# Three graph-convolution stages: slots' own rows loaded into the message tile first, gathered rows added to them by the indirect DMA

## The reference

```
def gcn_layer(h, W, b):
    hW = h @ W
    msg = norm * hW[row]                       # norm = dinv[row] * dinv[col]
    out = segment_sum(msg, col, num_segments=N)
    return out + b
h = relu(gcn_layer(x, W0, b0))                 # 128 -> 256
h = relu(gcn_layer(h, W1, b1))                 # 256 -> 256
h = gcn_layer(h, W2, b2)                       # 256 -> 128
x = layernorm(x + h)
```

## Time and profile before

| | us |
|---|---|
| median of 3 runs | 6531.18 (6519.85 to 6533.77) |
| the profiled execution, its own time | 6535.03 |
| its span in the trace | 6533.2 |
| first stage, from its first gather to the second stage's | 5422.0 to 5686.7 |
| second stage, likewise | 5686.7 to 6013.3 |
| third stage, to the end of the span | 6013.3 to 6533.2 |

### The profile page before, as it was taken

How to read it: one execution, slowest core, us unless ns; L and a number is a source line. 1 busy time by engine, 2 the same in 40 slices (tenths; PEclk the granted TensorE clock), 3 DMA queues, 4 the chain that set the end, 5 groups by cost and what they waited for, 6 DMA issues and landing times. The chain is left out here.

```text
span 6533.2 us, 85961 instructions
## 1 busy us (share of the span) xinstructions
PE 4769.7 (73%) x23527; PEld 3216.8 (49%) x23527; DVE 4268.8 (65%) x12858; ACT 3169.3 (49%) x7126; POOL 3968.9 (61%) x3991
## 2 busy tenths in 40 slices
PE   6899999889989843696435555556999996598221
PEld 4667776555558602596333333323666664465111
DVE  4788887433349745888895554556888886655554
ACT  3566665553346402554353455545888873364000
POOL 5566664654446477776676676674333336674777
PEclk9999999989999855696556776756999997799555
DMA  6999887887769623796556777765777776675332
GB/s 151 238 263 274 258 250 224 263 250 249 244 219 285 191 55 78 203 349 197 137 157 184 193 211 194 194 159 180 275 276 275 276 245 191 201 216 166 89 94 82
DMA packets 1135684, 1345.16 MB, mean 206 GB/s; under 512 B 137098, under 2 KB 822139, under 8 KB 1128938
## 3 DMA queue, kind: packets, MB, share of 16 engines
q1 hardware_dynamic: 1005066, 1085.70, 53.4%
q0 software_dynamic: 130144, 253.97, 16.1%
HBM read 659.31 MB, written 683.78 MB: 206 GB/s over the span
## 5 line engine op out<-in xcount | busy, mean ns | idle before, releaser
L1909 POOL DMA_INDIRECT jk_msg<-jk,idx_jk x588 | 554.8, 944 | 220.1 <-issue 174.1
L2173 POOL TENSOR_TENSOR rows_moved<-rows_x_in,w_lonely_row 128x512 f32<-128x512 f32 x98 | 152.5, 1557 | 561.3 <-DVE rows_x L722 537.0
L730 PE MATMUL jk_msg_ps<-ident,jk_msg 128*128 128x128 f32 x784 | 187.3, 383 | 418.8 <-DMA jk_msg<-jk,idx_jk 310.7
L1993 DVE TENSOR_TENSOR jk_msg_ps<-jk_msg_ps,jk_weight 128x512 f32<-128x512 f32 x196 | 137.1, 699 | 453.6 <-ACT jk_msg_ps L1948 343.8
L730 PEld LDWEIGHTS jk_msg_ps<-ident,jk_msg 128*128 128x128 f32 x784 | 123.9, 193 | 531.3 <-DMA jk_msg<-jk,idx_jk 410.0
L747 PE MATMUL sage_nodes_h_ps<-sage_nodes_h_t,w_ws 128*128 128x512 f32 x784 | 353.6, 594 | 0.0
L1930 PE MATMUL jk_h_ps<-jk_sum_t,w_jk_w 128*128 128x512 f32 x392 | 324.2, 923 | 27.9 <-DVE jk_sum_t L2010 26.5
L1249 DVE COPY sage_h<-sage_turn 128x512 f32<-128x512 f32 x98 | 67.7, 691 | 420.9 <-PE sage_turn L738 420.9
L2372 PE MATMUL gcn_end_sum_ps<-ident,gcn_end_rows 128*128 128x128 f32 x196 | 54.7, 434 | 384.4 <-DVE gcn_end_rows L2365 384.4
L945 ACT ACTIVATE sage_nodes_h_t<-sage_nodes_h_ps,w_b_c 128x512 f32<-128x512 f32 x392 | 247.7, 683 | 167.2 <-PE sage_nodes_h_ps L747 166.5
L610 POOL DMA_INDIRECT sage_msg<-h,idx x196 | 185.3, 945 | 230.9 <-ACT sage_weighted L1074 152.0
(11 more groups left out here) (455 smaller groups left out, 16104.9 us busy)
## 6 DMA issues: line engine op xcount, KB each, us to landing
h<-sage_nodes_h SPq DMA_DIRECT2D x196, 512.0 KB
h_t<-sage_h_t SPq DMA_DIRECT2D x98, 512.0 KB, 4.3
h<-sage_h SPq DMA_DIRECT2D x98, 512.0 KB, 3.5
jk_weight<-l_row SPq DMA_DIRECT2D x196, 256.0 KB
jk_t<-jk_h_t SPq DMA_DIRECT2D x196, 256.0 KB
rows_layers<-jk_t SPq DMA_DIRECT2D x49, 1024.0 KB, 5.8
r<-rows_h SPq DMA_DIRECT2D x98, 512.0 KB, 4.1
second_x_in<-u SPq DMA_DIRECT2D x147, 260.0 KB
```

What stands on the lines that cost most here:

```text
L730: mm = pe.transpose(ps[:, s * P:(s + 1) * P], rows[:, s, :], ident[:])
L1909: pool.indirect_dma_start(out=msg[:, j.number % deep, s, :], out_offset=None, in_=table, in_offset=bass.IndirectOffsetOnAxis(ap=index[:, g ...
L1993: dve.tensor_tensor(bank[:], bank[:], weight[:, j.number % 3, :], ALU.mult).then_inc(weighed.sem, 1)
L2173: pool.tensor_tensor(moved[:, g.b], x_in[:, g.number % 3], to_subs(W.lonely_row), ALU.add).then_inc(lonely_added.sem, 1)
```

## The change

The tiles `own` and `rows` and the function `vector_join` go. SP's own-row load now writes into `msg`; POOL waits for it, and then its four indirect DMAs add the gathered rows to what lies there. PE transposes straight from `msg` in the first and third stage; in the second ACT's `weigh` reads `msg` and writes a ring `rows` of two. `msg` has 8 buffers (6 in the second stage) and is freed by the transposes (by `weigh` in the second stage). SP issues the own loads further ahead.

```diff
+LOOP_DEEP, LOOP_DEEP_WIDE = 8, 6
@@ class LoopSums
-        self.depth, self.own_depth = DEEP if width == D else DEEP_WIDE, 3
+        self.depth = LOOP_DEEP if width == D else LOOP_DEEP_WIDE
...
-        self.own = ph.sb("own", [P, self.own_depth, SUB, width])
-        self.rows = ph.sb("rows", [P, 2, SUB, width])
...
+        self.scaled, self.freed = None, self.turned
+
+    def turn_from(self, rows, scaled):
+
+        self.rows, self.scaled, self.freed = rows, scaled, scaled
+
+    def sync_own(self, sp, g):
+        wait_for(sp, self.freed, g.lag(self.depth))
+        sp.dma_start(self.msg[:, g.number % self.depth], at(slot_rows(self.table), g)).then_inc(self.own_in.of(g), 16)
 
     def pool_fetch(self, pool, g):
-        pool_gather(pool, g, self.K.idx, self.joined, self.table, self.msg, self.arrived)
...
-    def vector_join(self, dve, g):
-        wait_for(dve, self.arrived, g)
-        wait_for(dve, self.own_in, g)
-        wait_for(dve, self.turned, g.lag(2))
-        dve.tensor_tensor(self.rows[:, g.b], self.msg[:, g.number % self.depth], self.own[:, g.number % self.own_depth], ALU.add).then_inc(self.joined.sem, 1)
...
+        wait_for(pool, self.own_in, g)
+        for s in range(SUB):
+            pool.indirect_dma_start(out=self.msg[:, g.number % self.depth, s, :], out_offset=None, in_=self.table,
+                                    in_offset=bass.IndirectOffsetOnAxis(ap=self.K.idx[:, cols(g, SUB, s, 1)], axis=0),
+                                    compute_op=ALU.add).then_inc(self.arrived.of(g), 16)
+
+    def tensor_turn(self, pe, g):
+        if self.scaled is None:
+            wait_for(pe, self.arrived, g)
+            rows = self.msg[:, g.number % self.depth]
+        else:
+            wait_for(pe, self.scaled, g)
+            rows = self.rows[:, g.b]
...
@@ gcn_first_block
-        run_groups(sp, EG, [(lambda g: sums.sync_own(sp, g), -2), (store, 2)])
+        run_groups(sp, EG, [(lambda g: sums.sync_own(sp, g), -6), (store, 2)])
...
@@ gcn_second_block
+    rows = ph.sb("rows", [P, 2, SUB, HID])
...
+    sums.turn_from(rows, weighed)
...
-        run_groups(sp, EG, [(lambda g: sums.sync_own(sp, g), -2), (store, 4)])
+        run_groups(sp, EG, [(lambda g: sums.sync_own(sp, g), -4), (store, 4)])
...
-            wait_for(act, sums.joined, g)
+            wait_for(act, sums.arrived, g)
+            wait_for(act, sums.turned, g.lag(2))
             for s in range(SUB):
-                ins = act.activation(sums.rows[:, g.b, s, :], sums.rows[:, g.b, s, :], ACT.Copy, scale=K.dinv[:, cols(g, SUB, s, 1)])
+                ins = act.activation(rows[:, g.b, s, :], sums.msg[:, g.number % sums.depth, s, :], ACT.Copy, scale=K.dinv[:, cols(g, SUB, s, 1)])
...
@@ gcn_end_block
-        run_groups(sp, EG, [(lambda g: sums.sync_own(sp, g), -2), (load_x, -1)])
+        run_groups(sp, EG, [(lambda g: sums.sync_own(sp, g), -6), (load_x, -1)])
```

More of the change, by code:

```diff
@@ L2343, in __init__ @@
         self.K, self.table, self.chunks = K, table, width // P
-        self.depth, self.own_depth = DEEP if width == D else DEEP_WIDE, 3
+        self.depth = LOOP_DEEP if width == D else LOOP_DEEP_WIDE
         self.msg = ph.sb("msg", [P, self.depth, SUB, width])
-        self.own = ph.sb("own", [P, self.own_depth, SUB, width])
-        self.rows = ph.sb("rows", [P, 2, SUB, width])
         self.sum_t = ph.sb("sum_t", [P, 2, self.chunks, GROUP])
         self.ps = [ph.ps(f"sum_ps{b}", [P, self.chunks, GROUP]) for b in range(2)]
-        self.arrived, self.own_in = ph.dma_sems("arrived", SUB, self.depth), ph.dma_sems("own_in", 1, self.own_depth)
@@ L2351, in __init__ @@
-        self.joined, self.turned = (ph.count_sem(n) for n in ("joined", "rows_turned"))
+        self.arrived, self.own_in = ph.dma_sems("arrived", SUB, self.depth), ph.dma_sems("own_in", 1, self.depth)
+        self.turned = ph.count_sem("rows_turned")
         self.chunk_summed, self.zeroed = ph.count_sem("chunk_summed", self.chunks), ph.sem("zeroed")
-    def pool_fetch(self, pool, g):
-        pool_gather(pool, g, self.K.idx, self.joined, self.table, self.msg, self.arrived)
-    def sync_own(self, sp, g):
-        wait_for(sp, self.joined, g.lag(self.own_depth))
-        sp.dma_start(self.own[:, g.number % self.own_depth], at(slot_rows(self.table), g)).then_inc(self.own_in.of(g), 16)
@@ L2361, in vector_join @@
-    def vector_join(self, dve, g):
-        wait_for(dve, self.arrived, g)
-        wait_for(dve, self.own_in, g)
-        wait_for(dve, self.turned, g.lag(2))
-        dve.tensor_tensor(self.rows[:, g.b], self.msg[:, g.number % self.depth], self.own[:, g.number % self.own_depth], ALU.add).then_inc(self.joined.sem, 1)
-    def tensor_turn(self, pe, g, ready):
-        wait_for(pe, ready, g)
+        self.scaled, self.freed = None, self.turned
+    def turn_from(self, rows, scaled):
+        self.rows, self.scaled, self.freed = rows, scaled, scaled
@@ L2371, in tensor_turn @@
             for c in range(self.chunks):
-                mm = pe.transpose(self.ps[g.b][:, c, s * P:(s + 1) * P], self.rows[:, g.b, s, c * P:(c + 1) * P], self.K.ident[:])
+                mm = pe.transpose(self.ps[g.b][:, c, s * P:(s + 1) * P], rows[:, s, c * P:(c + 1) * P], self.K.ident[:])
         mm.then_inc(self.turned.sem, 1)
@@ L2417, in make @@
             layer_rows(pe, h_ps[g.b], [(W.m["gcn0"], sums.sum_t[:, g.b])]).then_inc(made.sem, 1)
-        run_groups(pe, EG, [(lambda g: sums.tensor_turn(pe, g, sums.joined), 0), (make, 1)])
+        run_groups(pe, EG, [(lambda g: sums.tensor_turn(pe, g), 0), (make, 1)])
     @block.scalar
@@ L2439, in bias @@
             ins.then_inc(biased.sem, 1)
-        run_groups(dve, EG, [(lambda g: sums.vector_join(dve, g), -1), (lambda g: sums.vector_sum(dve, g, made), 0), (bias, 1)])
+        run_groups(dve, EG, [(lambda g: sums.vector_sum(dve, g, made), 0), (bias, 1)])
     ph.close()
@@ L2478, in make_y @@
             layer_rows(pe, lanes(y_ps[g.b], D), [(W.m["gcn2"], h_t[:, g.number % 3])]).then_inc(y_made.sem, 1)
-        run_groups(pe, EG, [(lambda g: sums.tensor_turn(pe, g, weighed), 0), (make_y, 3), (make, 1)])
+        run_groups(pe, EG, [(lambda g: sums.tensor_turn(pe, g), 0), (make_y, 3), (make, 1)])
     @block.scalar
@@ L2506, in _ @@
         sums.vector_zero(dve)
-        run_groups(dve, EG, [(lambda g: sums.vector_join(dve, g), -2), (lambda g: sums.vector_sum(dve, g, made), 0)])
+        run_groups(dve, EG, [(lambda g: sums.vector_sum(dve, g, made), 0)])
     ph.close()
@@ L2546, in turn @@
             turn_back(pe, lanes(rows_ps[g.b], D), sums.sum_t[:, g.b], range(SUB), K.ident).then_inc(back.sem, 1)
-        run_groups(pe, EG, [(lambda g: sums.tensor_turn(pe, g, sums.joined), 0), (turn, 1)])
+        run_groups(pe, EG, [(lambda g: sums.tensor_turn(pe, g), 0), (turn, 1)])
     @block.scalar
@@ L2570, in apply @@
             norm.vector_apply(dve, g, y, z, 4)
-        run_groups(dve, EG, [(lambda g: sums.vector_join(dve, g), -1), (lambda g: sums.vector_sum(dve, g, back), 0), (apply, 2), (add, 1)])
+        run_groups(dve, EG, [(lambda g: sums.vector_sum(dve, g, back), 0), (apply, 2), (add, 1)])
     ph.close()
```

## The result

The changed kernel takes 6821.7 us (median of 4 runs, 6816.2 to 6823.1) beside 6529.0 (4 runs): a ratio of 1.0449, 95% interval 1.043 to 1.0467. It is 293 us slower. The forecast was 6588 with a range to 6765; the direction was right, the size was not, by a factor of five: 57 us forecast, 293 measured.

A forecast was written before the change was run, and what follows sets the result against it. POOL's instruction stream was taken to bound the first and third stage, PE the second. Terms of -10.2 + 7.0 + 39 + 21 = +57 us gave 6588 beside a median of 6531, with an 8-in-10 range of 6524 to 6765.

The forecast's parts named there:

- Where the time is bound: POOL's instruction stream sets the first and third stage, PE at 6.1 us a group the second.
- Removed, -10.2 us: Joins gone from DVE: 9.0 us of stretched third-stage scatters, 0.5 of first-stage gathers, 0.7 of its last group's chain.
- Added at the starts, +7.0 us: POOL's first gather waits for the first own load: 2.4 us in first and third stage, net 2.2 in the second.
- Both small terms: Stretches and chain saved by dropping joins, and later stage starts, -10.2 and +7.0 us: -3 together.
- POOL's price of an add, +39 us: Each gather with add costs POOL 0.10 us more, on 392 gathers of the first and third stage; hidden in the second.
- The DMA engines, +21 us: Second stage: added rows cost the engines twice, 108% load, 6.6 us a group against PE's 6.1, over 43 groups.
- The wait on POOL in steady state, nothing: Own loads are issued 8 groups ahead (6 in the second stage), so POOL's wait for them costs nothing.
- Rivals: Other cases: adds cost nothing (6528, chance 0.30), adds cost much (6745 or 6781, 0.24), a gain (6515, 0.08).
- the large price: Adds cost POOL 0.47 us a gather, 6745, or the DMA engines four times per row, 6781; chance 0.24.

The follow-up runs named there:

- memset run: Changed kernel with plain gathers in place of adding ones, plus a POOL memset after each gather; 6725.9 us, ratio 1.0274 to the kernel before.
- run without adds: Changed kernel with its gathers as plain copies that overwrite the own rows, all else kept; 6536.0 us, ratio 0.9987 to the kernel before.
- join on PE: Kernel before, with the first and third stage's join moved from DVE to PE as two identity matmuls into PSUM; 6532.9 us, ratio 0.9981.
- form-by-form run: Kernel before with five POOL DMAs of each of twelve forms, plain and with add, put behind its end; 6665.9 us in one run.
- run with the doubled load: Changed kernel with plain gathers, SP loading each group's own rows a second time into a spare tile; 6523.8 us, ratio 0.9996 to the kernel before.

## Why the prediction was wrong, point by point

- **Where the time is bound**: right. POOL's stream in the first and third stage, PE's 6.1 us in the second. Stage times follow from POOL's period in every run, with that floor: 4 x 1.86 x 49 = 365 us of the first stage's 384.5, and likewise with 1.66 for the memset run.
- **Removed, -10.2 us**: about right. The 9.0 us of stretched scatters measured 8.6 in the run without adds and 8.4 in the join on PE. The first stage shows nothing larger than 0.3. One thing is finer than I wrote: not every scatter that starts while a join runs is stretched. In the third stage of the kernel before, the 18 long ones start 0.05 to 0.16 us after the join; 16 others start between 0.02 us before it and 0.04 after and keep their 1.00, and there it is the join that takes 0.70 to 0.76 in place of 0.69, as beside the scatter at 6060.82:

```profile
6060.78 0.76 DVE L2365 TENSOR_TENSOR gcn_end_rows<-gcn_end_msg,gcn_end_own 128x512 f32<-128x512 f32 x1 [5.35 <-DMA gcn_end_msg<-y,idx]
```
- **Added at the starts, +7.0 us**: about right. In the changed kernel the first gather follows SP's first issue by 3.3, 3.6 and 4.4 us where 3.0, 4.1 and 3.0 were assumed. In the second stage more came back than the join's 1.2 us: in the run without adds PE's first hidden-layer matmul follows the first gather by 16.4 us, where it was 20.7. Both small terms together: -8 us measured in the run without adds, -3 by my working.
- **POOL's price of an add, +39 us**: this is the step that failed. I took 0.10 us a gather and bounded it by 0.47; it is 0.61, which is 239 us in place of 39 over the first and third stage, and it lifts the second stage above PE's floor, where I had put nothing. Both values came from one assumption, that POOL's time goes by the entries it writes, so that a second read entry per row costs at most half again. The form-by-form run shows that rows are a small part of any gather (0.9 ns each, 0.12 of 0.94 us) and of the surcharge (1.1 ns each, 0.14 of 0.60). The rest is per instruction, which a ratio of entries can't bound; what POOL does in it stays open. The row that should have warned me was in the profile: 512 rows in 812 ns in a direct copy against 128 in 944 in a gather says that time does not go by rows between forms; I used it as a rate. With 0.61 in place of 0.10, and without the 21 us of the DMA engines, my own sum gives 392 x 0.61 = 239, in the second stage (7.44 - 6.1) x 49 = 66, and -3, so 302, beside 293 measured. (I had counted 43 groups in the second stage; the 67.9 us that it lost fit all 49 better, 66 against 58.)
- **The DMA engines, +21 us**: this term failed too, though it weighs little. The cost per row was sized well (1.9 times where I took 2; 2.4 in the first stage), the consequence was not. The engines reach 0.98 in the run with the doubled load and PE doesn't wait, and in the changed kernel they are not the limit: their term is covered there by POOL's 7.44 us a group.
- **The wait on POOL in steady state, nothing**: right; it occurs once a stage. One reading behind it was off: the 2.6 us a load at the start (13.05 us over five) held waits for joins, since `own` had three buffers; in the changed kernel the first eight loads take 5.59 us to issue.
- **Rivals**: the large price was the case that came, at 0.24, beyond its own figure for POOL (184 + 33). The range ended at 6765 because it was cut where 0.47 gave 6745.

The statement of the Trainium skill that I weighed, in "DMA: Bandwidth & Descriptors", section "Anatomy of one DMA — SWDGE (gpsimd) path", that many descriptors can be emitted before it shows, agrees with these runs as far as rows go: 0.9 ns each plain and 2.0 with add. Most of the loss came from the other part, the 0.45 us or so that a gather with add takes more whatever its rows.

The third stage's scatters over 1.1 us all begin inside a join, and so do the 27 such gathers of the second stage; in the third stage of the changed kernel, of the run without adds and of the join on PE, which have no join on DVE there, they vanish (longest 1.04 us). "SBUF — State Buffer" in the Trainium skill, section "Who interferes with whom", has a DVE instruction with two SBUF inputs contend with a GpSimd instruction that reads SBUF, and the join is one with two SBUF inputs. The same section reports that a `tensor_tensor` did not stall a DMA issued from GpSimd; here one did, 1.97 us in place of 0.95, and the measurement decides. That a port is what holds POOL no run here shows.

## What to carry to other kernels

Before moving work onto an engine, ask whether that engine's instruction stream is the pace of the stage: here DVE did the join for 8 us in all beside a POOL that had no gap, and each 0.1 us more per gather was 20 us in the first and in the third stage. A price that the trace doesn't show should be measured by a few instructions of each form at the end of the program; a bound built from one model of the cost is no bound. And an instruction off the critical path can still cost there by holding up an engine that is on it: taking the join away is worth 8 us here, if what replaces it goes to an engine that has room, PE, and not to the one that sets the pace.

## What the runs showed of the hardware that I had not expected

- An indirect gather with add costs POOL 1.35, 1.41 and 1.54 us for 32, 64 and 128 rows, a plain one 0.86, 0.90 and 0.94, at 512 as at 1024 bytes. A direct copy of 512 rows costs 0.78 plain and 1.31 with add (a fifth of five in a row; 1.44 between gathers). What POOL does in the fixed part was not looked into.
- The first two POOL DMAs after a change of form take 0.02 to 0.11 us longer each (1.06 and 1.00 after a direct copy, 0.99 after a gather with add, beside 0.95).
- A scatter that starts 0.05 to 0.16 us into a 0.69 us join on DVE takes 1.41 to 1.52 us. One that starts between 0.02 us before the join and 0.04 after takes 1.00, and the join up to 0.07 us more.
- The 16 DMA engines ran at a share of 0.98 and 303 GB/s for 210 us without PE missing anything, with stores, own loads and gathers in flight.
- With the add a gather is 144 packets in place of 32 or 48, and takes 2.4 (512-byte rows) and 1.9 times (1024) the engines' time.
- A POOL memset behind a gather starts at once and shortens the issue time ahead of the next gather from 0.30 to 0.17 us.
